# A graph attention layer on one core: the adjacency laid out load by load, and x normalised on three engines

## The chip, the cores and the metric

The kernel runs on one core of a Trainium2 chip. The metric is the time on the device, in microseconds (us), of one launch; lower is better. The engines are named as the profile names them: PE is TensorE (matmuls; PEld its weight loads), DVE is VectorE, ACT is ScalarE, POOL is GpSimd, and SP is the engine that issues most transfers and computes nothing here.

## The reference, cut to what matters

x has 4096 nodes of 128 features, adj is a 4096 x 4096 matrix of float32 that holds only 0 and 1. It is sparse, but for the first rows and columns (the hubs), where edges are frequent.

```python
def _L0_gnn_ref(x, adj, W, a):
    Wh = x @ W
    e_src = Wh @ a[:d_out]
    e_dst = Wh @ a[d_out:]
    e = jax.nn.leaky_relu(e_src[:, None] + e_dst[None, :], NEG_SLOPE)
    mask = (adj > 0) | jnp.eye(N, dtype=bool)
    e = jnp.where(mask, e, NEG_INF)
    alpha = jax.nn.softmax(e, axis=1)
    return alpha @ Wh
...
h = jnp.maximum(_layernorm(x, axis=-1), 0.0)
x = x + _L0_gnn_ref(h, adj, L0_gnn_W, L0_gnn_a)
h = jnp.maximum(_layernorm(x, axis=-1), 0.0)
x = x + _L1_gnn_ref(h, adj, L1_gnn_W, L1_gnn_B)
```

The second layer weighs neighbours by `where(adj < 1, sens(adj), 0)`. With entries of 0 and 1 alone all its weights are 0, so it adds nothing; the kernel verifies every entry of adj and has a general path, not entered here, for other values.

## The kernel before, in words

**Start.** x comes in eight octants of 512 rows. For each, DVE takes mean and variance (`moments`) and makes the scale and shift, ACT normalises the four blocks of 128 rows (L921), PE transposes them, ACT rectifies them on their way out of PSUM (L927), PE multiplies by W (and by the two score vectors), and ACT copies the product to `whe` (L935). GpSimd makes constants meanwhile, among them `pack_w` (powers of two on the diagonal). When all of `whe` is there, tables of row scores are made, the rows are scaled by their exponentials (`scale_rows`), and a table of all nodes is stored to DRAM (`node_table`).

**Stream.** adj is loaded in 32 chunks of 2 MB, each 512 rows (four planes of 128) by 1024 columns, in pieces of 4 KB, into a ring of six slots (`adj_ring`). chunk(i) belongs to super s = i // 8 (1024 rows), a group of columns c and a half h. SP issues the loads in order; a slot is loaded again when its chunk has been packed, checked and, in some, turned. For every chunk:

- `check(i)`: all entries are 0 or 1. DVE does it for 13 chunks in one instruction (L1134), ACT for 19 in two (L952, L961).
- `pack(i)` on PE (L642): eight rows become one word. The diagonal's squares are first cleaned by DVE (`clean_diagonal`, L1158, or `clear_diagonal`).
- `scan(step)` on DVE (L1172) finds the largest words of two chunks; `pick`, `decode` and `decode_shared` turn them, for a piece of several steps, into indices of neighbours.
- GpSimd gathers the neighbours' rows from `node_table` by index (L544), eight transfers of 128 rows in a group (four in two of them). Groups g0 to g9 are gathered in order, and a group waits only for its indices and for the scatter four groups earlier.
- `weigh(g)` on DVE (L1348 to L1387) makes the weights of group g when its rows have landed, and PE adds them up (`scatter`, L769).

**Hubs.** The first 128 columns of each half super (chunks with c = 0) are turned by PE (`turn_columns`, L609) into a PSUM bank; `column(i)` on DVE (L1442) multiplies them into `col_w`, reading the bank. The first 128 rows of adj are turned by PE too (`turn_hub`, L590), copied by ACT (`keep_hub`, L943), and weighed densely (`hub`, L1415).

**Order.** Each engine's program is a loop over i from 2 to 31, with tables that say at which i something is done (SCAN_AT, PICK_AT, WEIGH_AT and others). On DVE the turn of i = 8 contains pick(0), that of 9 decode(0). Checks in CHECK_LATE are done behind the scan of their turn: check(26) in the turn of 27, check(28) in that of 29.

**Tail.** After load 31: scan(15), pick(4), the last gathers, weigh(8), the last parts (L1468, L1472) and their stores.

Of the kernel before, what the change touches and what calls it, by code (L numbers as in the profile page):

```python
# [5 lines left out]
N, D, P = 4096, 128, 128  # L6
# [15 lines left out]
MOMENTS_AHEAD = 3  # L22
# [41 lines left out]
def is_diagonal(i):  # L64
    s, c, _ = chunk(i)
    return s == c
# [58 lines left out]
SCAN_AT = {2 * n + 2: n for n in range(STEPS - 1)}  # L125
# [22 lines left out]
def gnn_program(nc, x, adj, w0, a0, w1, b1, out):  # L148
# [4 lines left out]
    adj_chunks = adj.rearrange("(s h k p) (c n) -> s c h p k n", s=SG, h=2, k=HK, p=P, n=CW)  # L153
# [8 lines left out]
    with ctx:  # L162
# [18 lines left out]
        clean = sb("clean", [P, 2, HK, P], bf16)  # L181
# [8 lines left out]
        ident_bf = sb("ident_bf", [P, P], bf16)  # L190
# [108 lines left out]

        verdict = cand[:, 0:NBAD]  # L300
# [20 lines left out]
        def acc_of(s, t):  # L321
# [10 lines left out]
        stats_set, moments_set, std_set, rstd_set, shift_set, hn_done, hT_done, hT_copied = (  # L332
            sem(n) for n in ("stats_set", "moments_set", "std_set", "rstd_set", "shift_set", "hn_done", "hT_done", "hT_copied"))
# [6 lines left out]
        checked_v, signed, checked_a, diag_cleared, diag_clean, packed, scanned = (  # L340
            sem(n) for n in ("checked_v", "signed", "checked_a", "diag_cleared", "diag_clean", "packed", "scanned"))
        hub_turned, hub_kept, r_hub_set, hub_scaled, hub_w_set, hub_added, hub_rows_set, hub_spread = (
            sem(n) for n in ("hub_turned", "hub_kept", "r_hub_set", "hub_scaled", "hub_w_set", "hub_added", "hub_rows_set",
                             "hub_spread"))
        col_turned, hub_square_clear, col_w_set, col_added = (
            sem(n) for n in ("col_turned", "hub_square_clear", "col_w_set", "col_added"))
# [17 lines left out]
        judged, sign_judged, last_judged, bad_reduced, flag_set = (  # L364
            sem(n) for n in ("judged", "sign_judged", "last_judged", "bad_reduced", "flag_set"))
# [14 lines left out]
        def _(sp):  # L380
            def load_chunk(i):
                s, c, h = chunk(i)
                sp.dma_start(ring[:, i % AR, :].rearrange("p (k n) -> p k n", k=HK),  # L383
                             adj_chunks[s, c, h]).then_inc(adj_ready[i % AR], 16)
# [7 lines left out]
            for i in range(AR):  # L392
                load_chunk(i)
            for i in range(AR, CHUNKS):
                old = i - AR
                sp.wait_ge(packed, old + 1)
                if chunk(old)[1] == 0:
                    sp.wait_ge(col_turned, 2 * chunk(old)[0] + chunk(old)[2] + 1)
                if chunk(old)[0] == 0 and chunk(old)[2] == 0:
                    sp.wait_ge(hub_turned, old + 2)  # L400
# [4 lines left out]
                load_chunk(i)  # L405
# [1307 lines left out]
```

## Time and profile before

| | |
|---|---|
| median of 3 runs | 216.38 us (216.11 to 216.88) |
| the profiled execution: its time | 217.44 us |
| its span in the trace | 215.6 us |
| busiest engines | ACT 88%, DVE 84%, PE 72%, POOL 62% of the span |
| transfers of adjacency and x (queue q1) | 71.31 MB, 84.7% of what 16 engines could do in the span |
| HBM read | 74.06 MB, 363 GB/s over the span |
| mean granted clock of PE | 0.909 of full speed |

The profile shows one execution on the device. Its span goes from the first to the last instruction that the trace has; its time holds 1.84 us more, around the span. Times inside the trace count from the start of the span. A gain in the trace is a gain of the time, and is set against the profiled execution's own 217.44.

### The profile page before, as it was taken

What the parts mean: (1) busy time and instruction counts of PE and PEld (TensorE: products, weight loads), DVE (VectorE), ACT (ScalarE), POOL (GpSimd) and SP (SyncE); (2) the same over time, 40 slices, a digit from 0 to 9 for tenths busy, and PEclk for the clock granted to TensorE, in tenths of its full rate; (3) what the DMA queues carried; (4) which work ended last, traced back from release to release, by engine and by line L of the source; (5) the groups of instructions that cost most, each with busy time, mean ns of one, the idle gap of its engine ahead of it and who ended that gap; (6) DMA issues with size and microseconds to landing.
All of it is one profiled execution on the core that took longest, in us unless ns stands there. A gap on an engine that the chain in (4) does not pass through costs nothing.

```text
span 215.6 us, 3229 instructions
## 1 busy us (share of the span) xinstructions
PE 154.3 (72%) x956; PEld 103.7 (48%) x970; DVE 182.0 (84%) x535; ACT 189.3 (88%) x207; POOL 132.8 (62%) x140
## 2 busy tenths in 40 slices
PE   0186779983794992989929997499392977799472
PEld 0074565440362760549615844186341654668361
DVE  7993999999979999999488796995986499878855
ACT  0699987599899999999999999799999994999960
POOL 3980002295000588888878888888787788667450
PEclk9999999996599698599985999999979799999995
DMA  5999999999999999999999999999999999961303
GB/s 166 355 413 410 410 408 408 409 411 405 418 418 409 409 393 405 391 400 393 402 388 387 394 401 394 404 387 400 394 387 389 386 401 393 406 229 43 115 23 103
DMA packets 22259, 76.81 MB, mean 356 GB/s; under 512 B 2527, under 2 KB 3126, under 8 KB 22240
## 3 DMA queue, kind: packets, MB, share of 16 engines
q1 hardware_dynamic: 18912, 71.31, 84.7%
q0 software_dynamic: 2912, 5.22, 7.0%
q8 instruction: 8, 0.13, 0.2%
q10 hardware_dynamic: 416, 0.07, 0.2%
q14 instruction: 11, 0.09, 0.1%
HBM read 74.06 MB, written 4.23 MB: 363 GB/s over the span
## 4 chain that ended last, share of the span: by engine, by line
DMA 36%; DVE 31%; PE 18%; issue 7%; ACT 5%; SPq 1%; POOL 1%; POOLq 0%; DVEq 0%
DMA adj_ring<-in_adj 35%; DVE summed L1134 10%; PE bank L642 9%; DVE cand L1172 3%; ACT spread L921 3%; DVE hub_w L1415 3%; PE bank L769 2%; DVE x_sb L1458 2%; PE bank L754 2%; PE bank L761 2%; SPq L383 1%; DMA gathered_rows<-node_table,shared_index 1%; DVE stats L1114 1%; PE bank L629 1%; DVE shared_slots L1230 1%
## 5 line engine op out<-in xcount | busy, mean ns | idle before, releaser
L544 POOL DMA_INDIRECT gathered_rows<-node_table,index x48 | 76.0, 1584 | 36.5 <-DVE index L1309 22.5
L952 ACT ACTIVATE trash_a<-adj_ring,below_one 128x4096 fp8e4<-128x4096 f32 x19 | 70.4, 3705 | 5.7 <-DMA adj_ring<-in_adj 5.2
L642 PE MATMUL bank<-adj_ring,pack_w 128*128 128x512 bf16 (+3 forms) x255 | 70.0, 402 | 2.4 <-DMA adj_ring<-in_adj 1.5
L961 ACT ACTIVATE trash_a<-adj_ring 128x4096 fp8e4<-128x4096 f32 x19 | 68.7, 3614 | 0.5
L1134 DVE SCALAR_TENSOR_TENSOR summed<-adj_ring 128x4096 fp8e4<-128x4096 f32 x13 | 58.0, 4458 | 4.3 <-DMA adj_ring<-in_adj 4.2
L642 PEld LDWEIGHTS bank<-adj_ring,pack_w 128*128 128x128 bf16 x262 | 26.1, 104 | 31.5 <-issue 8.8
L544 POOL DMA_INDIRECT gathered_rows<-node_table,shared_index x24 | 33.2, 1382 | 9.6 <-issue 6.7
L1172 DVE MAX8 cand<-bank 128x8 f32<-128x120 f32 (+25 forms) x82 | 23.3, 351 | 3.9 <-PE bank L642 3.9
L769 PE MATMUL bank<-gathered_rows,spread 128*128 128x129 f32 x160 | 20.9, 282 | 3.9 <-DVE spread L1398 2.4
L769 PEld LDWEIGHTS bank<-gathered_rows,spread 128*128 128x128 f32 x160 | 19.4, 194 | 5.1 <-issue 4.8
L629 PE MATMUL bank<-codes,code_w 128*128 128x512 bf16 x25 | 11.2, 448 | 8.5 <-DMA adj_ring<-in_adj 5.6
L678 PE MATMUL bank<-whe,hub_w 128*128 128x129 f32 x64 | 10.4, 316 | 5.1 <-DVE hub_w L1419 5.0
L921 ACT ACTIVATE spread<-x_sb,shift,rstd 128x128 f32<-128x128 f32 x32 | 13.2, 497 | 0.3 <-DVE shift L1126 0.3
L678 PEld LDWEIGHTS bank<-whe,hub_w 128*128 128x128 f32 x64 | 9.1, 219 | 7.0 <-DVE hub_w L1419 6.8
L491 POOL PARTITION_ALL_REDUCE ends_all<-ends x1 | 1.4, 1442 | 17.3 <-DVE ends L1539 17.3
L565 PE MATMUL bank<-ident,spread 128*128 128x128 f32 x32 | 6.3, 327 | 7.8 <-ACT spread L921 7.8
L577 PE MATMUL bank<-w_sb,gathered_rows 128*128 128x130 f32 x64 | 9.8, 300 | 1.4 <-ACT whe L935 1.3
L1442 DVE SCALAR_TENSOR_TENSOR col_w<-r_rows,hub_whe,bank 128x512 f32<-128x512 f32 (+1 forms) x6 | 4.2, 708 | 7.4 <-PE bank L609 7.4
L629 PEld LDWEIGHTS bank<-codes,code_w 128*128 128x128 bf16 x32 | 3.7, 115 | 13.7 <-DMA adj_ring<-in_adj 6.2
L577 PEld LDWEIGHTS bank<-w_sb,gathered_rows 128*128 128x128 f32 x64 | 8.6, 208 | 2.7 <-ACT gathered_rows L927 2.4
L985 ACT ACTIVATE own_w<-ident,w_self 128x128 f32<-128x128 f32 x32 | 9.7, 386 | 0.0
L699 PE MATMUL bank<-slots,own_lane 128*32 128x16 f32 (+1 forms) x24 | 1.4, 188 | 10.5 <-issue 10.5
(190 smaller groups left out, 258.4 us busy)
## 6 DMA issues: line engine op xcount, KB each, us to landing
adj_ring<-in_adj SPq DMA_DIRECT2D x32, 2048.0 KB, 23.6
node_table<-gathered_rows POOLq DMA_DIRECT2D x4, 520.0 KB, 8.3
x_sb<-in_x SPq DMA_DIRECT2D x8, 256.0 KB, 5.9
out<-x_sb SPq DMA_DIRECT2D x3, 512.0 KB, 14.2
gathered_rows<-node_table,index POOLq DMA_INDIRECT x48, 5.9
gathered_rows<-node_table,shared_index POOLq DMA_INDIRECT x24, 5.4
out<-x_sb SPq DMA_DIRECT2D x2, 192.0 KB, 2.1
out<-x_sb SPq DMA_DIRECT2D x1, 128.0 KB, 1.9
```

What stands on the lines that cost most here:

```text
L544: pool.indirect_dma_start(out=rows[:, g % RING_GROUPS * GE + t, :], out_offset=None, in_=table, in_offset=bass.IndirectOffsetOnAxis(ap=row ...
L577: last = nc.tensor.matmul(bank[6 + half][:, b * (D + 2):(b + 1) * (D + 2)], hT[:, nb * P:(nb + 1) * P], w0_sb[:, :], start=(b == 0), stop= ...
L629: nc.tensor.matmul(to[:, :], code_w[:, 2 * c + half, :], codes[:, :], start=True, stop=False, skip_group_check=True)
L642: last = nc.tensor.matmul(to[:, lo:hi], pack_w[:, k, :], ring_hi[:, i % AR, row_at + lo:row_at + hi], start=False, stop=(k == KB - 1), ski ...
L678: last = nc.tensor.matmul(bank[7][:, 0:E1], hub_w[:, m % 2, b, :], whe[:, 4 * HUB_ORDER[m] + b, ONE:ONE + E1], start=(m + b == 0), stop=(m ...
L769: return nc.tensor.matmul(acc_of(SUPER_OF_GROUP[g], t), spread[:, g % 2, at * KB:(at + 1) * KB, :], rows[:, g % RING_GROUPS * GE + turn, G ...
L921: last = nc.scalar.activation(hn_block(b), x_sb[:, b, :], ACT.Identity, bias=shift[:, b:b + 1], scale=rstd[:, b:b + 1])
L952: nc.scalar.activation(trash_a[:, :], ring[:, i % AR, :], ACT.Sign, bias=below_one[:, :], scale=-1.0, accum_out=signs[:, n:n + 1], saturat ...
L961: nc.scalar.activation(trash_a[:, :], ring[:, i % AR, :], ACT.Abs, accum_out=sizes[:, n:n + 1], saturate=False).then_inc(checked_a, 1)
L985: last = nc.scalar.activation(own_w[:, t, :], ident[:, :], ACT.Copy, scale=w_self[:, nb:nb + 1])
L1134: nc.vector.scalar_tensor_tensor(trash_v, ring[:, i % AR, :], 1.0, ring[:, i % AR, :], ALU.is_ge, ALU.not_equal, accum_out=bad_v[:, n:n + ...
L1172: last = nc.vector.max(cand[:, at * 8:(at + 1) * 8], word_bank(step, half)[:, lo:hi])
```

## The change

The host lays adj out load by load, in the order in which it is read, as `adj_laid` with 33 loads. Load HUB stands between loads 2 and 3: the first 128 rows, already turned. In exchange the loads 0, 2, 4 and 6 lose their first plane (1.5 MB in place of 2 MB), so that the bytes are the same. The diagonal is set to zero in it and passed apart, as `adj_own` (128 x 32), which DVE checks by itself. In chunks with c = 0 the hub columns' squares stand turned at the end of the load. Loads are in two pieces per partition (8 KB, or 6 KB in loads of 1.5 MB), but for seven near the time at which the table is stored (4 and 3 KB).

So PE's turnings, ACT's keep_hub, and DVE's cleaning of the diagonal go. `column` reads the turned squares from the ring in SBUF and waits for the load. HUB is checked by ACT, whose second instruction writes `hub_mask`. DVE checks load 8 and no longer load 1, ACT load 1 and no longer load 8. At the start ACT normalises two blocks of four in each octant and POOL the other two; DVE rectifies octants 3 to 7; check(0) goes behind the scaling of rows.

```diff
+POOLED = 2
+RECTIFIED_V = [3, 4, 5, 6, 7]
...
+HUB = CHUNKS
+LOADS = [0, 1, 2, HUB] + list(range(3, CHUNKS))
+BESIDE_TABLE = range(4, 11)
...
+def first_plane(i):
+    return 1 if i != HUB and chunk(i)[0] == 0 and chunk(i)[2] == 0 else 0
...
+def runs_of(i):
+    return HK if LOADS.index(i) in BESIDE_TABLE else 2
...
-DVE_CHECKED = [0, 1, 2, 4, 6, 10, 11, 14, 18, 20, 22, 26, 28]
+DVE_CHECKED = [0, 2, 4, 6, 8, 10, 11, 14, 18, 20, 22, 26, 28]
...
-SCAN_AT = {2 * n + 2: n for n in range(STEPS - 1)}
+SCAN_AT = {2 * n + 2: n for n in range(1, STEPS - 1)}
...
+        def squares_of(i):
+            return ring[:, slot_of(i), HK * CW - (HK - first_plane(i)) * P:].rearrange("p (t n) -> p t n", t=KB)
...
+            for i, old in zip(LOADS[AR:], LOADS):
+                if old != HUB:
+                    sp.wait_ge(packed, old + 1)
+                    if chunk(old)[1] == 0:
+                        sp.wait_ge(col_w_set, 2 * chunk(old)[0] + chunk(old)[2] + 1)
                 if old in DVE_CHECKED:
                     sp.wait_ge(checked_v, DVE_CHECKED.index(old) + 1)
                 else:
                     sp.wait_ge(checked_a, ACT_CHECKED.index(old) + 1)
-                load_chunk(i)
+                load(i)
...
+            def normalise(o):
+                pool.wait_ge(shift_set, o + 1)
+                pool.wait_ge(rstd_set, o + 1)
+                if o >= 4:
+                    pool.wait_ge(hT_done, o - 3)
+                for b in range((o + 1) * BPO - POOLED, (o + 1) * BPO):
+                    last = nc.gpsimd.tensor_scalar(hn_block(b), x_sb[:, b, :], rstd[:, b:b + 1], shift[:, b:b + 1],
+                                                   ALU.mult, ALU.add)
+                last.then_inc(hn_done_pool, 1)
...
-                dve.wait_ge(col_turned, 2 * s + h + 1)
+                dve.wait_ge(adj_ready[slot_of(i)], landed(i))
                 first = 1 if s + h == 0 else 0
...
+                nc.vector.scalar_tensor_tensor(weights[:, :, lo:hi], r_rows[:, :, lo:hi], hub_whe[:, AQ:AQ + 1],
+                                               squares_of(i), ALU.max, ALU.mult).then_inc(col_w_set, 1)
...
-            for i in range(2):
-                check(i)
-
+            for o in range(2, XO):
+                moments(o)
+                deviation_inverse(o - 1)
+            rectify(3)
...
             for i in range(2, CHUNKS):
-                if i in CLEANED and i < 2 * CC + 2:
-                    clean_diagonal(i)
-                if i in DVE_CHECKED and i not in CHECK_LATE.values():
-                    check(i)
                 if i == 2:
                     scale_rows(1)
                     scale_rows(2)
-                if i == CLEARED:
-                    clear_diagonal(i)
+                    scan(0)
+                    check(0)
+                if i in DVE_CHECKED and i not in CHECK_LATE.values():
+                    check(i)
```

Three places show how the rows of an engine stand before and after. The first is DVE at the turn of i = 8, between the hub's weights and pick(0); `cand` are candidates of the scan, `slots` the picked ones. Before:

```order
L1419 TENSOR_TENSOR hub_w<-hub_w,hub_mask 128x512
L1158 TENSOR_TENSOR clean<-adj_ring,offdiag 128x512
L1442 SCALAR_TENSOR_TENSOR col_w<-r_rows,hub_whe,bank 128x8x64
L1172 MAX cand<-bank 128x8 x10
L1185 TENSOR_REDUCE fullest<-cand 128x1
L1191 MAX slots<-cand 128x8
```

And in the change:

```order
L1402 TENSOR_TENSOR hub_w<-hub_w,hub_mask 128x512
L1126 SCALAR_TENSOR_TENSOR summed,bad<-adj_ring 128x4096
L1421 SCALAR_TENSOR_TENSOR col_w<-r_rows,hub_whe,adj_ring 128x8x64
L1154 MAX cand<-bank 128x8 x10
L1167 TENSOR_REDUCE fullest<-cand 128x1
L1173 MAX slots<-cand 128x8
```

The clean of chunk 8's diagonal has gone, check(8) over 4096 columns stands in its place ahead of the scan and pick(0), and `col_w` reads the ring instead of a bank.

The second is DVE from weigh(5) to weigh(6), late in the stream: the weights of g5 (`same`, `spread`), column(26), check(26), column(27), scan(13), and the first row of weigh(6). Before:

```order
L1372 TENSOR_TENSOR spread<-same,hq_of_e 128x512 x2
L1442 SCALAR_TENSOR_TENSOR col_w<-r_rows,hub_whe,bank 128x8x64
L1134 SCALAR_TENSOR_TENSOR summed,bad<-adj_ring 128x4096
L1442 SCALAR_TENSOR_TENSOR col_w<-r_rows,hub_whe,bank 128x8x64
L1172 MAX cand<-bank 128x8 x5
L1348 TENSOR_TENSOR edge_w<-r_slots,gathered_rows 128x64
```

And in the change:

```order
L1354 TENSOR_TENSOR spread<-same,hq_of_e 128x512 x2
L1421 SCALAR_TENSOR_TENSOR col_w<-r_rows,hub_whe,adj_ring 128x8x64
L1126 SCALAR_TENSOR_TENSOR summed,bad<-adj_ring 128x4096
L1421 SCALAR_TENSOR_TENSOR col_w<-r_rows,hub_whe,adj_ring 128x8x64
L1154 MAX cand<-bank 128x8 x5
L1330 TENSOR_TENSOR edge_w<-r_slots,gathered_rows 128x64
```

The order is the same; what moved is the source of `col_w`, from the bank that PE's turning fills to the ring itself.

The third is SP's loads, between those of x and the stores. Before they are one row, `adj_ring<-in_adj 128x4x1024`, 32 times. In the change:

```order
L407 DMA adj_ring<-adj_laid 128x2x1536
L407 DMA adj_ring<-adj_laid 128x2x2048
L407 DMA adj_ring<-adj_laid 128x2x1536
L407 DMA adj_ring<-adj_laid 128x2x2048
L407 DMA adj_ring<-adj_laid 128x4x1024
L407 DMA adj_ring<-adj_laid 128x4x768
L407 DMA adj_ring<-adj_laid 128x4x1024
L407 DMA adj_ring<-adj_laid 128x4x768
L407 DMA adj_ring<-adj_laid 128x4x1024 x3
L407 DMA adj_ring<-adj_laid 128x2x2048 x22
```

24 loads are now of two pieces of 2048 elements for each partition, and the fourth is HUB.

## Rows read from the trace of the kernel before

**Rows 1.** The page's head: the span, busy time, and DMA by 40 slices.

```profile
span 215.6 us, 3229 instructions
...
PE 154.3 (72%) x956; PEld 103.7 (48%) x970; DVE 182.0 (84%) x535; ACT 189.3 (88%) x207; POOL 132.8 (62%) x140
...
DMA  5999999999999999999999999999999999961303
```

**Rows 2.** The chain of waits: start, duration, what; two pieces late in it.

```profile
139.17 26.24 DMA adj_ring<-in_adj
...
192.59 1.98 PE bank L642 x8
```

**Rows 3.** DVE's timeline, 164 to 195 us: start, duration, instruction, [idle before <-releaser].

```profile
164.16 1.34 DVE L1372 TENSOR_TENSOR spread<-same,hq_of_e 128x512 f32<-128x512 f32 x2
169.84 0.75 DVE L1442 SCALAR_TENSOR_TENSOR col_w<-r_rows,hub_whe,bank 128x512 f32<-128x512 f32 x1 [4.35 <-PE bank L609]
170.51 4.42 DVE L1134 SCALAR_TENSOR_TENSOR summed<-adj_ring 128x4096 fp8e4<-128x4096 f32 x1
...
176.78 0.20 DVE L1348 TENSOR_TENSOR edge_w<-r_slots,gathered_rows 128x64 f32<-128x64 f32 x1
...
190.98 0.43 DVE L1348 TENSOR_TENSOR same<-r_quad,gathered_rows 128x256 f32<-128x256 f32 x1 [0.41 <-DMA gathered_rows<-node_table,shared_index]
...
194.59 1.43 DVE L1172 MAX8 cand<-bank 128x8 f32<-128x272 f32 x4 [1.47 <-PE bank L642]
```

**Rows 4.** POOL's timeline, 71 to 186 us: gathers of groups g0 to g7.

```profile
71.75 1.15 POOL L544 DMA_INDIRECT gathered_rows<-node_table,index  x1 [19.76 <-DVE index L1309]
...
77.19 5.20 POOL L544 DMA_INDIRECT gathered_rows<-node_table,index  x1 [0.30 <-issue]
...
108.04 1.00 POOL L544 DMA_INDIRECT gathered_rows<-node_table,shared_index  x1 [0.30 <-issue]
...
115.84 1.61 POOL L544 DMA_INDIRECT gathered_rows<-node_table,index  x1 [0.30 <-issue]
...
166.08 1.00 POOL L544 DMA_INDIRECT gathered_rows<-node_table,index  x1 [0.30 <-issue]
...
171.29 4.50 POOL L544 DMA_INDIRECT gathered_rows<-node_table,shared_index  x1 [0.30 <-issue]
...
180.98 5.01 POOL L544 DMA_INDIRECT gathered_rows<-node_table,shared_index  x1 [0.30 <-issue]
```

**Rows 5.** DVE's timeline, 62 to 78 us: chunk 8, the first indices, a check.

```profile
62.93 0.69 DVE L1158 TENSOR_TENSOR clean<-adj_ring,offdiag 128x512 bf16<-128x512 f32 x1 [0.17 <-DMA adj_ring<-in_adj]
...
70.61 0.17 DVE L1309 SCALAR_TENSOR_TENSOR index<-words_i,empty_i 128x16 int32<-128x16 int32 x1
...
77.10 4.42 DVE L1134 SCALAR_TENSOR_TENSOR summed<-adj_ring 128x4096 fp8e4<-128x4096 f32 x1
```

**Rows 6.** Transfers, 13 to 36 us: the adjacency in pieces of 4 KB.

```profile
DMA packets 2375, 9.41 MB, mean 409 GB/s; under 512 B 79, under 2 KB 79, under 8 KB 2373
```

**Rows 7.** Transfers, 7.2 to 8.6 us: x in pieces of 2 KB.

```profile
DMA packets 293, 0.53 MB, mean 380 GB/s; under 512 B 33, under 2 KB 33, under 8 KB 293
```

**Rows 8.** ACT's groups of instructions by line, 0 to 32.1 us.

```profile
L921 ACT ACTIVATE spread<-x_sb,shift,rstd 128x128 f32<-128x128 f32 x32 | 13.2, 497 | 0.3 <-DVE shift L1126 0.3
```

**Rows 9.** SP's timeline, 34 to 60 us: loads into slots used before.

```profile
36.46 23.21 SPq L383 DMA_DIRECT2D adj_ring<-in_adj  x6
```

**Rows 10.** DVE's timeline, 106 to 118 us.

```profile
108.12 0.75 DVE L1442 SCALAR_TENSOR_TENSOR col_w<-r_rows,hub_whe,bank 128x512 f32<-128x512 f32 x1 [3.01 <-PE bank L609]
...
115.91 0.67 DVE L1158 TENSOR_TENSOR clean<-adj_ring,offdiag 128x512 bf16<-128x512 f32 x1
```

**Rows 11.** The page's DMA issues: count, median us from issue to landing.

```profile
gathered_rows<-node_table,index POOLq DMA_INDIRECT x48, 5.9
```

**Rows 12.** The timeline of all engines, 200 to 215 us: a gather in the tail.

```profile
205.97 1.11 POOL L544 DMA_INDIRECT gathered_rows<-node_table,shared_index  x1 [0.30 <-issue]
...
208.54 0.28 DVE L1387 SCALAR_TENSOR_TENSOR same<-r_oct,gathered_rows,shared_on 128x64 f32<-128x64 f32 x1 [0.56 <-DMA gathered_rows<-node_table,shared_index]
```

More of the change, by code:

```diff
@@ L380, in _, with load @@
         def _(sp):
[L381 to L384, printed above, removed]
+            def load(i):
+                lo = first_plane(i) * CW
+                laid = adj_laid[LOADS.index(i), 0:P * (HK * CW - lo)]
+                sp.dma_start(ring[:, slot_of(i), lo:HK * CW].rearrange("p (a n) -> p a n", a=runs_of(i)),
+                             laid.rearrange("(a p n) -> p a n", a=runs_of(i), p=P)).then_inc(adj_ready[slot_of(i)], 16)
             def store(s):
@@ L404, in _ @@
                     sp.wait_ge(checked_a, ACT_CHECKED.index(old) + 1)
-                load_chunk(i)
+                load(i)
             for s in range(SG - 1):
@@ L631, in pack @@
                     for k in ks:
[L632 to L644 removed]
+                        w = width(i) - BW if half == 0 else BW
+                        at = first * CW + (k % HK - first) * width(i) + half * (width(i) - BW)
+                        last = nc.tensor.matmul(to[:, BW - w:BW], pack_w[:, k, :], ring_hi[:, slot_of(i), at:at + w],
+                                                start=False, stop=(k == KB - 1), skip_group_check=True)
                 last.then_inc(packed, 1)
@@ L993, in _ @@
                     deviations(o + MOMENTS_AHEAD)
-                if o >= 1:
+                if o >= 1 and o - 1 not in RECTIFIED_V:
                     rectify(o - 1)
@@ L1041, in _ @@
                     own_weights(SG - 1)
+                if LOADS[LOADS.index(i) - 1] == HUB:
+                    check(HUB)
                 if i in ACT_CHECKED:
                     check(i)
-                if chunk(i)[0] == 0 and i % 2 == 0:
-                    keep_hub(i)
             def general_copies(tr, ev, t):
@@ L1409, in hub @@
                     dve.wait_ge(a_set, 1)
-                dve.wait_ge(hub_kept, 2 * (next(i for i in range(0, 2 * CC, 2) if chunk(i)[1] == n // 2) // 2) + n % 2 + 1)
+                if m == 0:
+                    dve.wait_ge(checked_a, ACT_CHECKED.index(HUB) + 1)
                 if m >= 2:
@@ L1696, with laid_out @@
 _INS = ["x", "adj", "L0_gnn_W", "L0_gnn_a", "L1_gnn_W", "L1_gnn_B"]
+def laid_out(arrays, np):
+    adj = arrays["in_adj"]
+    apart = adj.copy()
+    np.fill_diagonal(apart, 0)
+    laid = np.zeros((len(LOADS), P * HK * CW), adj.dtype)
+    for n, i in enumerate(LOADS):
+        if i == HUB:
+            block = apart[:P].reshape(P, CC, P, KB).transpose(2, 1, 3, 0)
+        else:
+            s, c, h = chunk(i)
+            rows = slice(s * HR + h * HK * P, s * HR + (h + 1) * HK * P)
+            block = apart[rows, c * CW:(c + 1) * CW].reshape(HK, P, CW).transpose(1, 0, 2)[:, first_plane(i):]
+            if c == 0:
+                squares = block[:, :, 0:P].reshape(LANES, KB, -1, P).transpose(3, 1, 2, 0)
+                block = np.concatenate([block[:, :, P:].reshape(P, -1), squares.reshape(P, -1)], axis=1)
+        block = block.reshape(P, runs_of(i), -1).transpose(1, 0, 2).reshape(-1)
+        laid[n, 0:block.size] = block
+    return {"adj_laid": laid, "adj_own": np.ascontiguousarray(np.diagonal(adj)).reshape(P, NB)}
 def kernel(**inputs):
```

255 lines of the change are left out of this document (98 added, 157 removed).

## The prediction

> **What bounds the kernel now.** I read the page's head first [rows 1]. ScalarE is the busiest engine (88%), and the DMA row shows the engines full from the second slice to the 35th (189 us) and nearly idle after the 36th. So there are two stages: a stream of 64 MiB, and a tail of some 23 us. The chain of waits [rows 2] then says what joins them: until 165.4 us it is a transfer of the adjacency, and before the tail PE packs load 31 at 192.59. The question is whether the data or something else decides when the tail starts.
>
> The rows around that seam [rows 3] answer it. VectorE waits 4.35 us for PE's turning of load 26 (169.84), checks load 26 (170.51), and comes to weigh(6), group g6, at 176.78 without waiting for its gathered rows. From there to the scan of the last step, at 194.59, are 17.81 us, with 0.41 us of waiting for group g7's rows and 1.47 us for PE. PE reaches load 31 in its program order, behind work that VectorE releases. So the tail starts when VectorE has passed weigh(6), load 31 has landed and g7 has landed, all within about 2 us. A gain in the stream alone is not a gain of the kernel.
>
> What feeds weigh(6) and weigh(7) is GpSimd's chain of gathers [rows 4]. It starts at 71.75, as soon as VectorE has made the first indices (70.61 [rows 5]), and goes on back to back, 1.00 us and 0.30 us apart, to 186 us. What VectorE adds to it is seen in the long ones: beside a check of 4.42 us (77.10 [rows 5]) the gather at 77.19 takes 5.20, and the gathers at 171.29 and 180.98 take 4.50 and 5.01. Nothing in this chain has time to spare, so a delay at its start arrives whole at its end.
>
> **The stream.** Rows of 4 KB move at 409 GB/s [rows 6], those of 2 KB, for x, at 380 [rows 7]. Over 16 engines that is 160.2 and 86.2 ns a piece. If time is linear in size, 12 ns are fixed in each, a piece of 8 KB takes 308 ns, and a load of 2 MB, 5.13 us now, saves 4% or 0.20 us. The window of x is short, so this is the upper end: 25 load equivalents (the 24 of 2 MB and two of 1.5 MB) save 0 to 5 us, and I take 3. By landing of load 8 only four of them have passed: 0.4 us. The bytes are the same. The Trainium skill (DMA: Bandwidth & Descriptors, Where 436 GB/s comes from) names 358 GB/s as the limit of the HBM side, by which larger pieces could bring nothing; the trace's 409 stands above it, so it disagrees.
>
> **The start.** Half of ScalarE's 32 normalising instructions (13.2 us for all [rows 8]) go to GpSimd and five of eight rectifyings to VectorE. The last projection could be ready some 5 us sooner, PE permitting. What that buys is room only: the first reuse of a ring slot is issued at 36.46 [rows 9] while six loads are queued. Afterwards the queue holds 1.5 MB less at that point (3.7 us at 409 GB/s), and slot 0 waits for VectorE's check(0), which now stands behind scale_rows(1), scale_rows(2) and scan(0). I put the stall of the stream between 0 and 2 us and take 0.4, which cancels the 0.4 gained by load 8: load 8 lands where it did. Each us more would delay everything by 1 us.
>
> **The first indices.** Here the change adds a wait to the gather chain. check(8), 4.42 us, moves from ScalarE in front of scan(3), pick(0) and decode(0) on VectorE; it can't start before load 8 lands (62.93, where the clean of load 8 starts now [rows 5]). Two cleans go, 0.69 us each with ends under the next instruction, so 1.2 in all. First index: 70.61 + 4.4 − 1.2 = 73.8, that is **+3.2 us** for the first gather. Nothing hides it: VectorE waits for load 8 already now (0.17 us at 62.93), and GpSimd for the index (19.76 us idle before 71.75 [rows 4]). The check of load 1 that VectorE loses in exchange lay at 21 to 30 us, where nothing waited.
>
> **Along the chain.** The cleans inside it go: the one at 115.91 [rows 10] makes the gather at 115.84 take 1.61 instead of 1.00; there are three, so at most −1.8. Against it, column now takes its squares from SBUF. With them in PSUM, col_w at 108.12 [rows 10] leaves the gather at 108.04 at 1.00. With two operands in SBUF it resembles the clean, of the same length: three before g6's end, 0 to +1.8. I take −0.5 net: **+2.7 us** at g6. As many checks as before fall on gathers: check(8) now lies ahead of the first one. The Trainium skill (SBUF — State Buffer, Who interferes with whom) says that a VectorE instruction with two SBUF inputs contends with a GpSimd instruction that reads SBUF, and one with a single SBUF input doesn't. The rows at 108.04 and 115.84 agree; by it the three would cost their full 1.8, and the net be 0 in place of −0.5.
>
> **Which group pays for check(26).** The wait of 4.35 us at col_w(26) goes, since column no longer needs PE's turning and load 26 (landed at 165.41, now or sooner) is there. VectorE ends weigh(5) at about 165.5 (164.16 + 1.34 [rows 3]), so check(26) starts near 166 instead of 170.51. Before, g6's last gather started at 166.08 and was past; afterwards it starts at 166.08 + 2.7 = 168.8. So check(26) now lies on a gather of g6, no longer of g7: +3.5 (4.50 less 1.00) to +4.2 (5.20 less 1.00), and I take 3.7. Last gather of g6: 166.08 + 2.7 + 3.7 = 172.5. From issue to landing take 5.9 us [rows 11]: 178.4. VectorE, which would be there at about 172.5, waits, and weigh(6) starts at 178.4 instead of 176.78: **+1.6 us**. Everything behind it (the epilogue, check(28), scan(14), pick(3), PE's packing of loads 30 and 31) is as long as before, so the scan of the last step and the tail move by 1.6.
>
> Gathers beside 8 KB pieces are not in the trace. Bounds: a gather at the end of the stream landed 4.99 us after GpSimd had issued it (180.98 + 5.01 to 190.98), one in the quiet tail 1.46 (205.97 + 1.11 to 208.54 [rows 12]). The stream adds up to 3.5, which 8 KB pieces could leave or at worst double: 0 to +3.5. I take 0, the nearest row being the same gather beside this stream. The Trainium skill (DMA: Bandwidth & Descriptors, Queues, rings and completion order) has an engine drain a whole packet of descriptors from one queue before it turns to another; by that, twice the bytes per descriptor would lean to the upper end, and 218.0 become 221.5.
>
> g7 doesn't decide: 186.0 + 2.7 = 188.7, then 1.5 to 5.0 us with the stream ending near 189.5, lands at 190.2 to 193.7, while VectorE now comes there at about 190.6 + 1.6 = 192.2.
>
> **Costed at nothing.** PE's turnings and diagonal pieces: PE waits for the stream. ScalarE has a twentieth check, and loses keep_hub and half of its early work; what it is late with is only the reuse of a slot, several loads ahead of landing. If that cover went, each us would delay a load by 1 us.
>
> **Sum.** +1.6 us on the profiled 217.44 (span 215.6): 219.0. The median of the runs is 1.06 lower, so 216.38 + 1.6 = 218.0. About 0.3%, 0.65 us, is what a measurement of this kernel can tell from no change.
>
> **Rivals.**
> The offsets cancel, 216.4, chance 0.2. col_w costs nothing and the cleans their full 1.8 (−1.3 against the sum), and check(26) or the landing is a few tenths short. For it: the gather at 108.04. Against: several terms must lie at their low ends.
>
> Faster, 214.9, chance 0.3. check(26) doesn't fall on g6, or check(8) hides in a start that is earlier than I think. Then g6 lands at 166.08 + 2.7 + 5.9 = 174.7, 2.1 sooner than weigh(6) stood, and load 31 three us sooner; g7, landing at about 191, still holds weigh(7), so the last scan starts 1.5 sooner: its 1.47 of waiting for PE is what goes. It decides where check(26) starts after about 168.8, or where the gather chain starts less than about 1 us late. With g7 on time too, the whole 3 us: 213.4. For it: weigh(5) depends on g5, which is 2.7 late too, and may push check(26) back. Against: col_w(26) and check(26) stand directly behind weigh(5), with 3 us to spare.
>
> Slower, chance 0.5, is my forecast: 218.0, own range 216.9 to 219.6; its upper part is gathers that land up to 1.6 later beside 8 KB pieces. A stall at slot 0 over 1 us would end on that side too.
>
> The range takes the middle of the faster case and half of the landing's bound: 214.6 to 219.6, with one in ten left out on each side. Faster by over 0.3%: 0.3; within: 0.2; slower: 0.5.
>
> **What would show it.** First gather at about 75 us; a long gather of g6 at 166 to 172 and none there in g7; weigh(6) with an idle time of several us before it, ended by the DMA of gathered rows; load 31 landed near 189.5, with PE packing it only at about 194. Wrong, if weigh(6) starts before 176, if the last scan waits for load 31 itself, or if the stream shows a gap near 38 us.

## The result, and the profile after

The changed kernel takes 224.88 us (median of 4 runs, 223.50 to 225.91) against 216.27 before: a ratio of 1.0389 (95% interval 1.0329 to 1.0448). It is slower by 8.6 us, where the prediction had 1.6 and a range that ended at 219.6. The profiled execution took 224.94 us, with a span of 223.0. Some executions of a kernel are over 1.5% longer than its fastest one: ratios and times below leave them out, and where a profiled execution is one of them, its own time stands beside what is read from it.

The page's head after, to set beside [rows 1]:

```profile
span 223.0 us, 3002 instructions
...
PE 151.4 (68%) x853; PEld 99.1 (44%) x865; DVE 177.7 (80%) x534; ACT 185.5 (83%) x183; POOL 137.2 (62%) x155
...
DMA  5999994899999999999999999999999999602312
GB/s 160 366 430 417 409 406 185 272 401 379 422 417 425 422 417 405 415 408 408 401 412 396 400 417 405 407 401 405 411 393 400 414 399 400 262 11 42 113 23 100
```

Every engine that computes is busy for less time than before, but GpSimd. The DMA row has a hole in its seventh and eighth slice (185 and 272 GB/s, 33 to 45 us) that wasn't there. The transfers of 34 to 44 us, in 40 slices of 0.25 us, show it closer:

```profile
DMA  9999986543210000000000099028969999899998
GB/s 406 393 406 406 393 340 234 184 160 123 86 49 37 12 0 0 0 0 0 0 0 0 0 131 131 0 33 246 197 229 377 393 426 475 344 377 377 426 492 360
```

The rate begins to fall at 35.3 us, is nil from 37.5 to 39.8, and is whole again only at 41.5. That gap is the sign of being wrong that the prediction had named ("if the stream shows a gap near 38 us"). What the loads waited for is told by three engines' timelines (start, duration, instruction; [idle before <-releaser]). First DVE, with check(0) and check(2):

```profile
35.44 3.34 DVE L1126 SCALAR_TENSOR_TENSOR summed<-adj_ring 128x3072 fp8e4<-128x3072 f32 x1
...
38.90 3.36 DVE L1126 SCALAR_TENSOR_TENSOR summed<-adj_ring 128x3072 fp8e4<-128x3072 f32 x1
...
67.06 4.42 DVE L1126 SCALAR_TENSOR_TENSOR summed<-adj_ring 128x4096 fp8e4<-128x4096 f32 x1 [5.71 <-DMA adj_ring<-adj_laid]
...
78.71 0.17 DVE L1284 CAST words_i<-bank 128x16 int32<-128x16 f32 x1 [1.09 <-PE bank L704]
...
79.00 0.18 DVE L1291 SCALAR_TENSOR_TENSOR index<-words_i,empty_i 128x16 int32<-128x16 int32 x1
```

ACT, with both halves of check(1), and the second half of HUB's:

```profile
32.02 3.70 ACT L939 ACTIVATE trash_a<-adj_ring,below_one 128x4096 fp8e4<-128x4096 f32 x1
...
35.84 3.62 ACT L948 ACTIVATE trash_a<-adj_ring 128x4096 fp8e4<-128x4096 f32 x1
...
43.75 3.62 ACT L948 ACTIVATE hub_mask<-adj_ring 128x4096 fp8e4<-128x4096 f32 x1
```

And PE, waiting for the loads 4 and 5:

```profile
37.96 0.39 PE L634 MATMUL bank<-codes,code_w 128*128 128x512 bf16 x1 [1.66 <-DMA adj_ring<-adj_laid]
...
46.90 2.74 PE L639 MATMUL bank<-adj_ring,pack_w 128*128 128x512 bf16 x6 [6.12 <-DMA adj_ring<-adj_laid]
```

The sixth load in the queue (load 4) is there at 37.96. Slot 0 comes free with check(0) at 38.8, slot 1 with check(1) at 39.5, slot 2 with check(2) at 42.3, HUB's slot at 47.4, and load 8 is the one that waits for HUB's. So load 5, issued at 38.8 into an empty queue, takes 8.1 us to 46.90 (at 409 GB/s its 2 MB take 5.1), and load 8 is there at 67.06 instead of 62.93 [rows 5].

From there the delay goes down the chain of gathers of [rows 4]. The gathers after; the third of these lines is the first of g5:

```profile
80.15 1.17 POOL L577 DMA_INDIRECT gathered_rows<-node_table,index  x1 [28.13 <-DVE index L1291]
...
142.76 1.50 POOL L577 DMA_INDIRECT gathered_rows<-node_table,index  x1 [0.30 <-issue]
...
157.90 1.00 POOL L577 DMA_INDIRECT gathered_rows<-node_table,shared_index  x1 [0.31 <-issue]
...
171.49 4.70 POOL L577 DMA_INDIRECT gathered_rows<-node_table,index  x1 [0.30 <-issue]
...
176.49 1.00 POOL L577 DMA_INDIRECT gathered_rows<-node_table,index  x1 [0.30 <-issue]
```

The first starts 8.40 us later than before (71.75), g6's last 10.41 later (166.08). The seam on DVE, to set beside [rows 3]:

```profile
168.37 0.29 DVE L1330 TENSOR_TENSOR same<-r_pair,gathered_rows 128x128 f32<-128x128 f32 x1 [0.64 <-issue]
...
170.90 4.42 DVE L1126 SCALAR_TENSOR_TENSOR summed<-adj_ring 128x4096 fp8e4<-128x4096 f32 x1
...
182.44 0.23 DVE L1330 TENSOR_TENSOR edge_w<-r_slots,gathered_rows 128x64 f32<-128x64 f32 x1 [5.18 <-issue]
...
192.67 1.49 DVE L1154 MAX8 cand<-bank 128x8 f32<-128x24 f32 x5 [1.80 <-PE bank L639]
...
198.18 0.42 DVE L1330 TENSOR_TENSOR same<-r_quad,gathered_rows 128x256 f32<-128x256 f32 x1
...
202.06 1.43 DVE L1154 MAX8 cand<-bank 128x8 f32<-128x272 f32 x4 [1.74 <-PE bank L639]
```

check(26) stands on a gather of g6 (171.49, 4.70 us). VectorE waits 5.18 us before weigh(6), which starts 5.95 us after g6's last gather began on GpSimd. The profile puts this wait down to "issue"; that it is for g6's rows is read from other runs: weigh(6) starts 4.95 us after that gather has ended here, and 4.5 to 5.1 us after it in b1, e1, e8 and e10, at times that differ by 5.6 us. weigh(6) is 5.66 us later than before, the last scan 7.47, the end of the span 7.4: the tail is as long as it was.

### The profile page after: what moved, and what is told of

The parts are those of the page before. It is cut to its first block, busy times and chain, and to the rows that moved or that the text cites. A ratio compares the mean times of both kernels' runs of the same rounds, so it can differ in the third digit from the quotient of the medians.

```text
span 223.0 us, 3002 instructions
## 1 busy us (share of the span) xinstructions
PE 151.4 (68%) x853; PEld 99.1 (44%) x865; DVE 177.7 (80%) x534; ACT 185.5 (83%) x183; POOL 137.2 (62%) x155
## 4 chain that ended last, share of the span: by engine, by line
POOL 22%; issue 21%; DVE 17%; PE 13%; DMA 13%; ACT 12%; POOLq 1%; DVEq 0%
POOL gathered_rows L577 19%; DMA adj_ring<-adj_laid 9%; ACT trash_a L939 5%; PE bank L639 3%; DMA gathered_rows<-node_table,index 3%; PE bank L617 2%; DVE summed L1126 2%; PE bank L767 2%; DVE x_sb L1437 2%; PE bank L752 2%; ACT hub_mask L948 2%; ACT trash_a L948 2%; DVE shared_slots L1212 1%; DMA gathered_rows<-node_table,shared_index 1%; DVE cand L1154 1%
## 5 line engine op out<-in xcount | busy, mean ns | idle before, releaser
L577 POOL DMA_INDIRECT gathered_rows<-node_table,index x48 | 77.8, 1620 | 46.8 <-DVE index L1291 32.8
L939 ACT ACTIVATE trash_a<-adj_ring,below_one 128x4096 fp8e4<-128x4096 f32 x20 | 74.0, 3702 | 5.2 <-DMA adj_ring<-adj_laid 4.2
L639 PE MATMUL bank<-adj_ring,pack_w 128*128 128x512 bf16 (+1 forms) x239 | 69.3, 422 | 8.2 <-DMA adj_ring<-adj_laid 7.1
L1126 DVE SCALAR_TENSOR_TENSOR summed<-adj_ring 128x4096 fp8e4<-128x4096 f32 (+1 forms) x13 | 54.7, 4207 | 9.2 <-DMA adj_ring<-adj_laid 5.7
L577 POOL DMA_INDIRECT gathered_rows<-node_table,shared_index x24 | 28.2, 1177 | 9.8 <-issue 6.7
L634 PE MATMUL bank<-codes,code_w 128*128 128x512 bf16 x29 | 13.2, 454 | 5.8 <-DMA adj_ring<-adj_laid 5.6
L697 PEld LDWEIGHTS bank<-slots,own_lane 128*32 128x32 f32 x24 | 1.3, 138 | 17.7 <-issue 17.7
L1398 DVE TENSOR_SCALAR hub_w<-r_hub,whe 128x128 f32<-128x128 f32 x32 | 8.8, 354 | 0.0
L491 POOL TENSOR_SCALAR spread<-x_sb,rstd,shift 128x128 f32<-128x128 f32 x16 | 7.2, 456 | 2.2 <-DVE shift L1112 2.0
L962 ACT ACTIVATE r_rows<-bank 128x512 f32<-128x512 f32 x8 | 4.5, 590 | 4.7 <-PE bank L665 4.6
```

Of the source, the lines that this page charges most:

```text
L577: pool.indirect_dma_start(out=rows[:, g % RING_GROUPS * GE + t, :], out_offset=None, in_=table, in_offset=bass.IndirectOffsetOnAxis(ap=row ...
L634: nc.tensor.matmul(to[:, :], code_w[:, 2 * c + half, :], codes[:, :], start=True, stop=False, skip_group_check=True)
L639: last = nc.tensor.matmul(to[:, BW - w:BW], pack_w[:, k, :], ring_hi[:, slot_of(i), at:at + w], start=False, stop=(k == KB - 1), skip_grou ...
L939: nc.scalar.activation(trash_a[:, :], ring[:, slot_of(i), :], ACT.Sign, bias=below_one[:, :], scale=-1.0, accum_out=signs[:, n:n + 1], sat ...
L1126: nc.vector.scalar_tensor_tensor(trash_v[:, first_plane(i) * CW:HK * CW], data, 1.0, data, ALU.is_ge, ALU.not_equal, accum_out=bad_v[:, n: ...
L1398: last = nc.vector.tensor_scalar(hub_w[:, m % 2, b, :], r_hub[:, :], whe[:, nb, QA:QA + 1], whe[:, nb, AA:AA + 1], ALU.mult, ALU.max)
```

## The experiments

Ratios are to the kernel before, with their 95% interval; times in us are medians, and 1% is 2.2 us. Edits are to the changed kernel where nothing else is said.

**Two delays, apart and together.** e1 moves check(0):

```diff
+            check(0)
             dve.wait_ge(ends_reduced, 1)
...
                     scan(0)
-                    check(0)
```

> The changed kernel, with check(0) moved ahead of the scaling of rows, into VectorE's 2.46 us of waiting for GpSimd's reduction. Theory A (the gap of about 4 us in the stream at 37 us, in which slot 0 waits for check(0), is handed on to load 8, to the first gather and so to the end): load 8 lands at about 63 instead of 67.06, the first gather starts at about 76 instead of 80.15, time about 220.7. Rival B (the stream recovers the gap anyway, since it ends at about the same time as before, and the loss lies in the late chain, where PE's clock is low): stream earlier, time within 1 us of 224.9.

e2 changes who checks load 8:

```diff
-DVE_CHECKED = [0, 2, 4, 6, 8, 10, 11, 14, 18, 20, 22, 26, 28]
+DVE_CHECKED = [0, 2, 4, 5, 6, 10, 11, 14, 18, 20, 22, 26, 28]
```

> The changed kernel, with check(8) given back to ScalarE and check(5) taken by VectorE in its place, where it idles 3.3 us; the gap in the stream stays. Theory A: load 8 still lands at about 67, the first gather starts 3.7 us sooner, at about 76.4, time about 221. Rival C (ScalarE, with check(8) in its row again, becomes late and holds slots): the first gather is sooner, and the time stays above 223.

e3 has both edits, and f3 is e3 again.

> Both edits together: check(0) early and check(5) in place of check(8). Theory A: the two delays add up, first gather at about 72, g6 still held by check(26), weigh(6) at about 174.5, time 214 to 216.5. Rival B: above 220. Rival D (pieces of 8 KB make gathers land later, so the chain is late anyway): first gather at 72, weigh(6) after 177, time about 219.

> The kernel with check(0) early and check(5) in place of check(8) once more, with more rounds, beside the last two on one chip: its ratio to the kernel before was 0.9965 (0.9926 to 1.0003). Expected 0.994 to 1.000; above the first of these three by 1 us if the rest of the gap counts.

Measured: e1 1.0167 (1.0071 to 1.0263), 220.7 us from two runs, 219.62 and 221.81; e2 1.0065 (1.0025 to 1.0104), 218.3; e3 0.9965 (0.9926 to 1.0003), 215.9, and again 0.9981 (0.9948 to 1.0013), 216.2. So check(0) early gives 2.2% alone and 1.0% beside e2; check(8) away gives 3.2% alone and 2.0% beside e1. Both together take the whole 3.9% back, and no more. e1's time is the one that theory A gave, but its interval is wide. In its profiled execution, of 223.75 us, load 8 lands at 65.04 and the first gather starts at 78.11, half of the way to 63 and 76, since half of the gap stays; f3, with the same early check(0), moves 13.03 MB in 30 to 64 us. The transfers in that time, after and then in e1:

```profile
DMA packets 3274, 11.75 MB, mean 346 GB/s; under 512 B 160, under 2 KB 160, under 8 KB 3272
```

```profile
DMA packets 3594, 13.00 MB, mean 382 GB/s; under 512 B 175, under 2 KB 175, under 8 KB 3592
```

Before it was 13.98 MB. So the gap is 2.23 MB after and 0.98 in e1, 5.4 and 2.4 us at 409 GB/s. In e2 the first gather starts 6.8 us sooner, where 3.7 had been expected and check(8) takes 4.4, and the time is below 223; rival C is out. The scan ahead of pick(0), and the first gather, in e2:

```profile
63.52 1.68 DVE L1154 MAX8 cand<-bank 128x8 f32<-128x56 f32 x10 [0.48 <-PE bank L639]
```

```profile
73.31 1.17 POOL L577 DMA_INDIRECT gathered_rows<-node_table,index  x1 [19.90 <-DVE index L1291]
```

The first indices need loads 0 to 7 only. Scan and pick now run while load 8 is still landing (67.00), and only PE's placing, behind its packing of load 8, waits for that. check(8) in front of them had put scan and pick behind load 8 as well, as the clean of load 8 did in the kernel before [rows 5].

**One part of the change in the kernel before.** b1:

```diff
-DVE_CHECKED = [0, 1, 2, 4, 6, 10, 11, 14, 18, 20, 22, 26, 28]
+DVE_CHECKED = [0, 2, 4, 6, 8, 10, 11, 14, 18, 20, 22, 26, 28]
...
-            for i in range(2):
-                check(i)
+            check(0)
```

> The kernel before, with only one part of the change: VectorE checks load 8 in place of load 1, and ScalarE load 1. Theory A: no gap in the stream (six loads queued until 42 us), first gather at about 75.5 instead of 71.75, g7's rows and so weigh(7) about 3.5 us later, time 218 to 220. Rival E (the chain of gathers has room, so its start doesn't matter): 216.3 within 0.7.

Measured: 1.0149 (1.0080 to 1.0219), 220.6 us. Its gathers:

```profile
77.90 1.14 POOL L544 DMA_INDIRECT gathered_rows<-node_table,index  x1 [26.53 <-DVE index L1309]
...
169.75 4.03 POOL L544 DMA_INDIRECT gathered_rows<-node_table,index  x1 [0.30 <-issue]
```

Rival E is out: the chain's start matters. But the start is 6.15 us later, not 3.7: load 1's check on ScalarE makes a small gap here too (load 8 at 64.22, 1.3 us later than before), and check(26) moves onto g6 in this kernel as well (169.75, 4.03 us).

**The gap filled by leaving checks out.** e8 and e9 leave loads 0 and 1 unverified; e9 has e2's edit too.

```diff
+UNCHECKED = [0, 1]
...
-                else:
+                elif old in ACT_CHECKED:
                     sp.wait_ge(checked_a, ACT_CHECKED.index(old) + 1)
```

> The changed kernel without check(0) and check(1): these two loads go unverified. Slots 0 and 1 then wait for the packing alone. Theory A: no gap in the stream at 37 us, load 8 lands at about 62.5 instead of 67.06, first gather at about 75.5, time about 220.5 (the gap of 5.4 us costs 4 to 5). Rival: the gap comes back at the next slot (HUB's check on ScalarE), time above 223.

> As the last one (loads 0 and 1 unverified), and VectorE checks load 5 instead of load 8. What the change is worth with both delays away: first gather at about 71 or sooner, stream ending 3 us sooner than before the change, time 213 to 215. Rival (the late chain of VectorE and PE is the bound, whatever the stream does): 216 within 0.7.

Measured: e8 1.0159 (1.0105 to 1.0212), 219.1 us; e9 0.9887 (0.9840 to 0.9934), 214.2. The transfers of e8, 30 to 64 us:

```profile
DMA packets 3823, 13.93 MB, mean 410 GB/s; under 512 B 176, under 2 KB 176, under 8 KB 3821
```

And its first gather:

```profile
75.65 1.18 POOL L578 DMA_INDIRECT gathered_rows<-node_table,index  x1 [24.81 <-DVE index L1292]
```

The gap is gone, as is the rival, and with it 2.3% of the time, some 5 us: load 8 at 62.56, the first gather 4.5 sooner. This is the price of the stall to about a us; the two checks that were left out also lighten VectorE by 3.3 us and ScalarE by 7.3.

**check(26).** e10 leaves load 26 unverified; e5 is e3 with check(26) behind column(27).

```diff
-CHECK_LATE = {22: 22, 27: 26, 29: 28}
+CHECK_LATE = {22: 22, 29: 28}
+CHECK_MID = {28: 26}
...
                     column(i - 1)
+                if i in CHECK_MID:
+                    check(CHECK_MID[i])
                 if i in SCAN_AT:
```

> The changed kernel without check(26): load 26 goes unverified. Measures the term of check(26) on g6: no long gather in g6, its rows 3.7 us sooner, weigh(6) at 178.7 instead of 182.44, time 221 to 222. Rival (g6 is late for its start alone, and VectorE has 5 us to wait there anyway): less than 1 us.

> The kernel with both edits, and check(26) put behind column(27) instead of ahead of it, so that it starts when g6's last gather has been issued. If check(26) on a gather of g6 is what holds weigh(6): no long gather in g6, weigh(6) at about 175.5 instead of 177, time 1 to 2 us below 216.0. Rival: weigh(6) is held by the start of the chain alone, time within 0.7 of 216.0.

Measured: e10 1.0159 (1.0126 to 1.0192), 219.8 us; e5 0.9991 (0.9945 to 1.0037), 217.2. The first gather of g5 and the last of g6 in e10, and its weigh(6):

```profile
156.67 1.00 POOL L578 DMA_INDIRECT gathered_rows<-node_table,shared_index  x1 [0.30 <-issue]
...
171.47 1.00 POOL L578 DMA_INDIRECT gathered_rows<-node_table,index  x1 [0.30 <-issue]
```

```profile
177.56 0.23 DVE L1331 TENSOR_TENSOR edge_w<-r_slots,gathered_rows 128x64 f32<-128x64 f32 x1 [3.60 <-issue]
```

It starts 4.9 us sooner, and the time is 2.3% shorter: check(26) on g6 is on the path. Of the 4.9 us, 1.2 are there before g5, where the edit can't act (156.67 against 157.90), so check(26) itself is worth some 3.7, the price that was predicted. In e5 (profiled execution 220.67 us) no gather of g6 stands on check(26), and yet nothing is won; the expectation for e5 failed. What holds weigh(6) there is that the edit put check(26) behind column(27), which waits for load 27:

```profile
171.48 0.75 DVE L1422 SCALAR_TENSOR_TENSOR col_w<-r_rows,hub_whe,adj_ring 128x512 f32<-128x512 f32 x1 [5.13 <-DMA adj_ring<-adj_laid]
172.15 4.42 DVE L1127 SCALAR_TENSOR_TENSOR summed<-adj_ring 128x4096 fp8e4<-128x4096 f32 x1
...
177.76 0.24 DVE L1331 TENSOR_TENSOR edge_w<-r_slots,gathered_rows 128x64 f32<-128x64 f32 x1
```

So e5 exchanged one wait for another, and doesn't show what check(26) costs where the chain starts in time.

**Pieces of 8 KB.** e11 is the changed kernel, e4 is e3, with this edit:

```diff
-    return HK if LOADS.index(i) in BESIDE_TABLE else 2
+    return HK
```

> The changed kernel with all loads in pieces of 4 KB and 3 KB. Theory A (its end hangs on the chain of gathers, not on the stream): load 8 lands within 0.5 us of 67, gathers take as long from issue to landing (5.9 us median), time within 1 of 224.9. Rival D (8 KB pieces hold the gathers): landings sooner by 1 us or more and time 1 to 3 lower. Rival F (the stream binds here too): 2 to 3 higher.

> The kernel with both edits (check(0) early, check(5) in place of check(8)), and all loads in pieces of 4 KB (3 KB in loads of 1.5 MB) as before the change. What the larger pieces are worth: by the rates of the changed kernel (408 GB/s at 80 to 120 us, 395 before) the stream ends about 3 us later. Theory A (the late chain is held by gathers and VectorE, not by the stream): load 8 lands less than 1 us later, time 216 to 217.5. Rival D (pieces of 8 KB slow the gathers' landing): gathers land sooner, weigh(6) with them, time below 215.

Measured: e11 1.0449 (1.0401 to 1.0496), 225.3 us; e4 1.0108 (1.0053 to 1.0163), 218.7. The windows of 80 to 120 us (busy time of PE, PEld, DVE, ACT, POOL, then the granted clock, the DMA share and GB/s), after and then in e11:

```profile
80.00:120.00 40.00, 30.51 (x179) 20.48 (x181) 37.26 (x91) 30.60 (x20) 33.76 (x21) 0.88 1.02 408
```

```profile
80.00:120.00 40.00, 31.55 (x181) 20.89 (x181) 37.10 (x89) 30.83 (x20) 33.91 (x21) 0.88 1.03 397
```

And the gathers' issues, median to landing, after and then in e11:

```profile
gathered_rows<-node_table,index POOLq DMA_INDIRECT x48, 5.9
```

```profile
gathered_rows<-node_table,index POOLq DMA_INDIRECT x48, 6.1
```

Larger pieces speed the stream by 2.8% and don't delay gathers: rival D is out, twice. What that is worth hangs on what binds: in the changed kernel 0.6%, inside the two intervals, and in e3 1.3 to 1.4%, some 3 us. There theory A was wrong: with the gather chain in time, the stream binds again. The last packing and the last scan in e4, and then the scan in f3:

```profile
193.07 1.98 PE L639 MATMUL bank<-adj_ring,pack_w 128*128 128x512 bf16 x8 [0.92 <-DMA adj_ring<-adj_laid]
```

```profile
195.09 1.43 DVE L1154 MAX8 cand<-bank 128x8 f32<-128x272 f32 x4 [1.93 <-PE bank L639]
```

```profile
192.34 1.43 DVE L1154 MAX8 cand<-bank 128x8 f32<-128x272 f32 x4
```

In e4 PE waits for load 31 itself, and VectorE for PE; in f3 neither waits there.

**The start.** e7 gives all normalising and rectifying back to ScalarE (POOLED = 0, RECTIFIED_V = [], without the calls and waits of the other engines).

> The changed kernel with ScalarE normalising and rectifying all of x, as before the change (GpSimd and VectorE do none of it). The last projection is ready at about 32 instead of 26.4 us, check(0) with it, so the gap in the stream grows by about 5 us: first gather at about 85, time 228 to 230. Rival: another wait holds slot 0 and the shared start buys nothing, time within 1 of 224.9.

e6 lets VectorE check loads 0 and 1, both ahead of the reductions of the scores, and ScalarE load 8.

> The changed kernel with the checks dealt out as before the change (VectorE checks loads 0 and 1, ScalarE load 8), both ahead of the reductions of the scores, at about 25 us. If the gap in the stream comes only from slots 0 and 1 waiting for checks: no gap at 37 us, load 8 lands at about 62.5, though the tables are made some 6 us later; first gather at about 71, time 213.5 to 216. Rival: the later tables (scale_rows, store of the table) hold the first gather instead, time above 217.

Measured: e7 1.0436 (1.0381 to 1.0492), 226.4 us; e6 1.0163 (1.0107 to 1.0219), 220.1. When the scores are reduced in e7:

```profile
30.62 0.56 DVE L1514 TENSOR_REDUCE ends<-whe 128x1 f32<-128x32 f32 x4 [7.08 <-ACT whe L927]
```

After, it is 26.45, so sharing is worth 4.2 us there, 2.3 at load 8 (69.33), and 0.5% in time, which the intervals don't part from nothing. That is less than the 3 to 5 us expected: check(0) starts only 2.2 us later in e7 (37.61). In e6 both checks are done by 32.4, and yet the gap is nearly whole: 12.06 MB in 30 to 64 us. PE waits there for VectorE's products of the scores, which stand behind the checks, and packs load 0 only then:

```profile
33.52 1.19 PE L646 MATMUL bank<-hub_w,same_lane 128*128 128x256 f32 x2 [5.90 <-DVE hub_w L1525]
...
34.93 1.49 PE L639 MATMUL bank<-adj_ring,pack_w 128*128 128x512 bf16 x3 [0.22 <-issue]
```

So the expectation failed in its condition: slot 0 waits for the check and the packing, and the later of the two leaves the gap. e6 also has check(8) away, as e2 has, and its first gather starts at 72.97; why it is still 1% slower than e2 stays open.

**A complete kernel that uses this.** f1: check(0) as in e1, check(1) on VectorE ahead of scale_rows(1), check(8) on ScalarE. f2 is f1 with check(5) on VectorE too.

```diff
-DVE_CHECKED = [0, 2, 4, 6, 8, 10, 11, 14, 18, 20, 22, 26, 28]
+DVE_CHECKED = [0, 1, 2, 4, 6, 10, 11, 14, 18, 20, 22, 26, 28]
...
+            check(0)
             dve.wait_ge(ends_reduced, 1)
...
                 if i == 2:
+                    check(1)
                     scale_rows(1)
                     scale_rows(2)
                     scan(0)
-                    check(0)
```

> Complete kernel, all loads verified: check(0) in VectorE's wait for the reduction, check(1) on VectorE ahead of the scaling of rows, check(8) on ScalarE. Theory A (what is left of the gap, 1 MB, comes from slot 1, which waits for ScalarE's check(1) until 39.4 us): almost no gap, load 8 at about 62.5 to 63.5, first gather at 70 to 71, time 214 to 215.5, and faster than the kernel before by 0.5 to 1%. Rival: later tables or ScalarE, with check(8) and HUB, hold another slot, time 216 or more.

> As the last one, and VectorE also checks load 5 in the time in which it idles ahead of load 6, so ScalarE has one check less. If ScalarE's row holds slots between 45 and 60 us: 0.5 to 1 us below the last one. If VectorE has no idle time left there: the same or slower by up to 1 us.

Measured: f1 0.9930 (0.9902 to 0.9958), 215.1 us, faster than the kernel before by 0.7%; f2 1.0096 (1.0058 to 1.0134), 218.1. In the profiled execution of f1, of 217.67 us, the stream has no gap at 37 to 43 us, but a shallow one from 44 to 54 us, where SP waits for later checks; over 30 to 64 us it moves 13.11 MB, little more than e1, and load 8 lands at 64.30, not at 62.5 to 63.5. So slot 1 was what was left of the gap at 41 us, and filling it moved the wait on. f2 has 14 checks on VectorE; its profiled run is one of 215.8, the others lie at 217.6 to 219.5, and no trace of those is here, so why it is slower than f1, by more than either expectation had, stays open.

## Why the prediction was right in direction and wrong in size

**Right.** The seam was read rightly: the tail starts when VectorE has passed weigh(6), and what feeds it is the chain of gathers from the first index on. check(26) moved from g7 to g6, at the predicted price (4.70 − 1.00 = 3.7 us), and e10 shows it on the path. weigh(7) didn't wait.

**Right by luck.** check(26) was to start near 166, ahead of g6's last gather, because the wait at col_w(26) goes. It started at 170.90, later than before: weigh(5), in front of it, began at 168.37, 4.9 us later than before, since VectorE had waited for g3's rows (3.98 us before 147.37) and for g5's (0.64 us); the rival "Faster" had named that ("may push check(26) back"). check(26) met g6 only because the gathers were later still. Where the chain is in time, the predicted reason holds: in f3 check(26) starts at 164.38, and g6's last gather (164.72) takes 4.95 us.

**Also right.** Gathers land beside 8 KB pieces as beside 4 KB. The stream's pieces gave 3.3% at 80 to 120 us (408 GB/s against 395 before), near the 4% of the upper end. The Trainium skill (DMA: Bandwidth & Descriptors, Queues, rings and completion order) has an engine drain a packet of descriptors before it turns to another queue; medians of 5.9 us with 8 KB and 6.1 with 4 KB show nothing of a longer wait.

**The step that failed** is in the start: "I put the stall of the stream between 0 and 2 us and take 0.4, which cancels the 0.4 gained by load 8: load 8 lands where it did." The stream lost 5.4 us in moved bytes, and load 8 landed 4.13 us later. The step compared neither time that it needed: when the queue runs dry (the rate is nil at 37.5 us, and load 4 is there at 37.96) and when check(0) ends (38.8). Their distance, about a us, lies inside the 0 to 2. What it left out: the rate falls 2.5 us before the last load is whole; the load issued into the empty queue took 8.1 us, where the stream delivers one in 5.1; and the next three slots hung on checks too (39.5, 42.3, 47.4), one on VectorE and two on ScalarE, behind one another. I looked at slot 0 alone, and put ScalarE's checks at nothing ("several loads ahead of landing"); b1 shows 1.3 us at load 8 for the move of check(1) to ScalarE. e8 shows what the checks of loads 0 and 1 cost in the changed kernel, some 5 us.

With load 8's 4.1 us in the sum, weigh(6) would have stood at 182.5, where it is (182.44), and the time at about 222. Of the 7.5 us between the two profiled executions (the one before lay 1.1 above its median), 1.6 were forecast, 4.1 are load 8's, and 1.8 lie behind weigh(6).

**Sizes of the other terms.** That the sum to weigh(6) comes out so closely is luck in part, since two terms were off against each other. Without load 8's 4.13 us, the first gather was 4.27 later, not 3.2: the second clean lay ahead of decode(0), in the wait for PE's placing, which now shows as 1.09 us at 78.71, so that taking it out gave nothing. Against the kernel before, check(8) costs about its duration; e2's 6.8 us are more, because without the clean and without check(8) nothing in front of scan and pick needs load 8. Along the chain it was −1.7 (10.41 − 8.40 − 3.70), not −0.5: three cleans gave 1.5, the col_w from SBUF took 0.6, nearly all of it on one gather (142.76, 1.50 us), and three checks fell on the gathers of g3 and g4 so that they held them 0.6 less, which the prediction hadn't counted. Behind weigh(6), "is as long as before" missed 1.8 us: from weigh(6) to the last scan are 19.62 us, not 17.81, with 1.80 of waiting for PE in scan(14). PE's columns at that place take 3.78 us, where they took 2.02 before (180.93). After, with the window of their stretch, and then the window before:

```profile
186.68 3.78 PE L752 MATMUL bank<-hub_whe,hub_w 128*128 128x129 f32 x16 [6.27 <-DVE x_sb L1437]
```

```profile
186.68:190.46 3.78, 3.78 (x17) 3.66 (x18) 3.78 (x1) 3.75 (x4) 3.56 (x1) 0.50 1.00 397
```

```profile
180.93:182.95 2.02, 2.02 (x16) 1.95 (x18) 2.02 (x1) 0.69 (x1) 1.97 (x1) 1.00 1.04 408
```

The granted clock of these columns is 0.50, the level of 1.2 GHz, and was 1.00, that of 2.4 GHz. From 176 to 187 us PE had been busy for 3.84 of 11 us, behind the late weigh(6), with a mean of 0.72 granted; before, for 7.96 of the same 11 us, all at 1.00. That the idle time brought the clock down is read from these rows and not tested by a run.

**The rivals.** "Faster, 214.9" named the two things that decide, check(26) off g6 and the chain's start less than 1 us late. With the start in time and the stream unbroken the time is 214.2 (e9, two loads unverified), and 215.1 in f1, which is complete; so the change has a gain of about 0.7% in it, and the places of its checks cost the rest.

The prices are not additive: 5 us for the gap (e8), 7 for check(8) (e2), some 4 for check(26) (e10), where the loss is 8.6; e1 and e2, 2.2% and 3.2% apart, give 3.9% together. With the chain in time something else holds the end: load 27 in e5, the stream in e4.

## What to carry to other kernels

Where a stream runs through a ring, compute for every slot of the first turn when it comes free and when the queue runs dry, and add the time from issue to landing: here a queue that was empty for two us, with the slots behind it late as well, cost five. Before moving work onto an engine that is ahead of a chain without slack, follow the first link of that chain, since a delay there is handed on to the end. And after a change that makes an engine come earlier, look what its long instructions now fall on.

## What the runs showed of the hardware

A gather that begins while VectorE runs an instruction with two operands in SBUF is held to about 0.87 us after that instruction's end. check(26) ends at 175.32, and the gather at 171.49 at 176.19. column's product of 0.75 us at 142.64 holds the gather at 142.76 to 1.50. One that began well before such an instruction isn't held: the gather at 93.71, 0.64 us ahead of check(11), took 1.00. Within a tenth of a us of the start both are found: 170.16, 0.07 ahead of column's product, took 1.02, while in the kernel before the gather at 115.84, 0.07 ahead of the clean, was held to 0.87 us after the clean's end [rows 10]. The Trainium skill (SBUF — State Buffer, Who interferes with whom) has the two contend; these rows agree, and add that it is the gather's beginning that decides. So an instruction of about 0.7 us costs between nothing and 0.6.
